# Attention context computed token by token, normalised once a layer, then transposed

## The reference, cut to what matters

```python
scores = jnp.einsum('bqhd,bkhd->bhqk', q, k) / scale     # layer 0: causal mask
attn = jax.nn.softmax(scores, axis=-1)
out = jnp.einsum('bhqk,bkhd->bqhd', attn, v).reshape(b, s, H * HS)
return out @ W_proj + b_proj
```

## Time and profile before

| what | us |
|---|---|
| median of 3 runs | 873.56 (868.95 to 879.3) |
| the profiled execution, its own time | 875.49 |
| its span, first to last instruction | 873.8 |
| mean granted TensorE clock in it | 0.846 of full |
| OPENING / FIRST / STEADY / STEADY / LAST / CLOSING, by barriers | 113.5 / 179.5 / 189.5 / 191.5 / 129.5 / 70.3 |

### The profile page before, as it was taken

One profiled execution on the slowest core, in us unless ns is written; L12 is line 12 of the kernel. 1 busy time (PEld: TensorE's weight loads), 2 busy tenths in 40 slices (PEclk: granted clock), 3 DMA queues, 4 the chain that ended last, 5 costly groups with the idle time before them and its releaser, 6 DMA issues. The chain is left out here.

```text
span 873.8 us, 8707 instructions
## 1 busy us (share of the span) xinstructions
PE 640.4 (73%) x3156; PEld 429.7 (49%) x3156; DVE 547.7 (63%) x936; ACT 307.6 (35%) x576; POOL 215.3 (25%) x184
## 2 busy tenths in 40 slices
PE   2479556835677787858778778857787888896697
PEld 2233234423223574646346565645345657765596
DVE  4749656576998547765997556757995355442211
ACT  2324031234331132653543223563442424442131
POOL 4429511212343101031543101132452011001000
PEclk9989965757888678888899788878998899998789
DMA  6985000354670000373660003273630000000000
GB/s 143 299 170 151 0 9 1 47 145 113 161 172 25 9 1 10 48 201 93 161 152 10 9 0 38 71 191 93 175 92 9 1 1 1 1 1 10 0 1 10
DMA packets 26641, 61.69 MB, mean 71 GB/s; under 512 B 4928, under 2 KB 12752, under 8 KB 26608
## 3 DMA queue, kind: packets, MB, share of 16 engines
q1 hardware_dynamic: 26608, 61.26, 30.2%
HBM read 53.52 MB, written 3.54 MB: 65 GB/s over the span
## 5 line engine op out<-in xcount | busy, mean ns | idle before, releaser
L1895 POOL TENSOR_TENSOR state<-state,C_rows 128x1024 f32<-128x1024 f32 x42 | 113.1, 2692 | 178.4 <-DVE state L1445 156.8
L1445 DVE TENSOR_TENSOR_SCAN state<-decay,dx_rows 128x512 f32<-128x512 f32 x72 | 105.8, 1510 | 9.9 <-PE py L980 6.9
L980 PE MATMUL py<-state,sel 128*96 128x512 f32 x168 | 91.9, 681 | 14.8 <-POOL state L1895 14.6
L1765 ACT ACTIVATE decay<-d_rows,a_neg 128x255 f32<-128x255 f32 x144 | 61.1, 496 | 94.5 <-DMA d_rows<-delta_dram 58.8
L1052 PE MATMUL pd<-w_dn,act 128*128 128x192 f32 x480 | 90.5, 343 | 3.7 <-ACT act L1778 3.7
L1052 PEld LDWEIGHTS pd<-w_dn,act 128*128 128x128 f32 x480 | 82.7, 200 | 7.1 <-ACT act L1778 4.6
L1036 PE MATMUL pu<-fT,w_up 128*128 128x256 f32 x180 | 65.9, 452 | 12.4 <-ACT act L1778 11.9
L1438 DVE TENSOR_TENSOR dx_rows<-dx_rows,B_rows 128x1024 f32<-128x1024 f32 x36 | 58.4, 1621 | 12.5 <-DMA dx_rows<-delta_x_dram 12.5
L792 PE MATMUL ps<-hT,w_qkv 96*96 96x256 f32 x128 | 41.5, 495 | 33.4 <-DVE hT L1583 32.7
L1936 POOL TENSOR_TENSOR cT<-cT,inv_den 128x256 f32<-128x256 f32 x24 | 19.9, 831 | 174.3 <-DVE inv_den L1642 174.3
L1778 ACT ACTIVATE act<-pu,b_up 128x256 f32<-128x256 f32 x90 | 37.7, 470 | 71.3 <-PE pu L1040 71.1
(11 more groups left out here) (285 smaller groups left out, 1220.0 us busy)
## 6 DMA issues: line engine op xcount, KB each, us to landing
dx_rows<-delta_x_dram SPq DMA_DIRECT2D x41, 512.0 KB, 5.1
d_rows<-delta_dram SPq DMA_DIRECT2D x36, 512.0 KB, 6.6
d_rows<-delta_x_dram SPq DMA_DIRECT2D x6, 512.0 KB, 5.1
w_dn<-exp_w_dram SPq DMA_DIRECT2D x1, 2304.0 KB
B_rows<-xdbl SPq DMA_DIRECT2D x4, 512.0 KB, 7.0
C_rows<-xdbl SPq DMA_DIRECT2D x4, 512.0 KB, 10.7
w_up<-exp_w_dram SPq DMA_DIRECT2D x1, 1536.0 KB
delta_x_dram<-delta_x SPq DMA_DIRECT2D x4, 384.0 KB, 3.4
```

The costliest lines, as they stand in the source:

```text
L980: mm = nc.tensor.matmul(py[0:INNER, :], sel[:, first:first + INNER], flat(states[g % held])[:, paths], start=False, stop=(g == GROUPS - 1) ...
L1445: ins = nc.vector.tensor_tensor_scan(flat(states[g % held])[:, both], flat(decay[g % 2])[:, both], dx_rows[g % 2][:, both], 0.0, ALU.mult, ...
L1765: ins = nc.scalar.activation(decay[g % 2][:, k, rest], d_rows[g % 2][:, k, rest], ACT.Exp, scale=a_neg[:, at:at + 1])
L1895: nc.gpsimd.tensor_tensor(now, now, C_rows[:, :], ALU.mult).then_inc(sc_done, 1)
```

## The change

The context is formed with tokens on the partitions. The stationary operand is a 128x128 tile of `probs` (keys x queries), the moving one 17 columns of `v_aug` (16 values and the ones). A head takes four products in layer 1 and three in the causal layer 0. All 24 x 17 columns of a layer stay in `pm` (408 of 512). After the last unit DVE takes one reciprocal of the 24 sums of each token and one product over 128x384; PE transposes the result with `turn`; DVE and ACT copy one half each to `cT`; the projection has two chunks of 96 rows. Gone are `den_sel`, `spread`, `context_copy`, `invert_sums`, `context_scale`, two memsets of `w_o`, and six of eight loads of `w_o`.

```diff
-            for j in range(QUAD):
-                b_loads.append((w_o[l][32 * j:32 * j + HEAD, :, :], w_heads[j]))
+            b_loads.append((w_o[l][:, :, :], t[f"w_o{l}"].rearrange("(c p) n -> p c n", p=CGROUP)))
...
                         def context(u):
                             pe.wait_ge(p_done[l], u + 1)
-                            if u in (2, 4):
-                                pe.wait_ge(den_inv[l], u // 2)
                             for j in range(2):
                                 head = 2 * u + j
-                                row = 32 * (head % QUAD)
-                                for kt in range(TILES):
-                                    q0 = 128 * kt if causal else 0
-                                    mm = nc.tensor.matmul(pm[row:row + 32, q0:TOKENS], v_aug[:, kt, head, :],
-                                                          probs[u % 2][:, j, kt, q0:TOKENS], ...
+                                for i in range(TILES):
+                                    out = pm[:, (HEAD + 1) * (HEADS * i + head):(HEAD + 1) * (HEADS * i + head + 1)]
+                                    tiles = range(i + 1 if causal else TILES)
+                                    for kt in tiles:
+                                        mm = nc.tensor.matmul(out, probs[u % 2][:, j, kt, 128 * i:128 * (i + 1)],
+                                                              v_aug[:, kt, head, 0:HEAD + 1],
+                                                              start=(kt == 0), stop=(kt == tiles[-1]))
...
-                            if u in (2, 4):
-                                spread(u // 2 - 1)
                             others((l, 2 * u + 1))
                         context(UNITS - 1)
                         others((l, "context"))
-                        spread(HTILES - 1)
+                        pe.wait_ge(ctx_done[l], 1)
+                        turn(pm, ps[:, 3, :], ctx_tok, CHALF).then_inc(ctx_turned[l], 1)
                         others((l, "spread"))
-                        pe.wait_ge(ctx_done[l], HTILES)
+                        pe.wait_ge(ctx_copied[l], 2)
                         for tl in range(TILES):
-                            for ht in range(HTILES):
-                                mm = nc.tensor.matmul(ps[:, 2, WIDTH * tl:WIDTH * (tl + 1)], ...
+                            mm = chunks(ps[:, 2, WIDTH * tl:WIDTH * (tl + 1)],
+                                        lambda c: cT[0:CGROUP, c, 128 * tl:128 * (tl + 1)],
+                                        lambda c: w_o[l][:, c, :])
...
+                        def normalise():
+                            dve.wait_ge(av_done[l], UNITS)
+                            context = pm[:, 0:TILES * HEADS * (HEAD + 1)].rearrange("p (t d) -> p t d", d=HEAD + 1)
+                            link(nc.vector.reciprocal(inv_den[:, :], context[:, :, HEAD]))
+                            nc.vector.tensor_tensor(
+                                ctx_tok[:, :, :].rearrange("p t (h d) -> p (t h) d", d=HEAD), context[:, :, 0:HEAD],
+                                inv_den[:, :].unsqueeze(2).to_broadcast([128, TILES * HEADS, HEAD]),
+                                ALU.mult).then_inc(ctx_done[l], 1)
...
-                            if u in (2, 4):
-                                context_copy(u // 2 - 1)
...
-                            if u in (2, 4):
-                                invert_sums(u // 2 - 1)
...
-                        context_copy(HTILES - 1)
+                        normalise()
                         others((l, "context"))
-                        invert_sums(HTILES - 1)
+                        dve.wait_ge(ctx_turned[l], 1)
+                        nc.vector.tensor_copy(cT[0:CGROUP, 0, :], pm[0:CGROUP, 0:TOKENS]).then_inc(ctx_copied[l], 1)
                         others((l, "spread"))
... (ACT)
                         others((l, "context"))
+                        sc.wait_ge(ctx_turned[l], 1)
+                        nc.scalar.activation(cT[0:CGROUP, 1, :], ps[0:CGROUP, 3, 0:TOKENS], ACT.Copy
+                                             ).then_inc(ctx_copied[l], 1)
                         others((l, "spread"))
... (POOL)
-                        if run_a and at in (5, 9, "spread"):
-                            context_scale(l, {5: 0, 9: 1, "spread": 2}[at])
```

More of the change, by code:

```diff
@@ L29 @@
 HEADS, HEAD = 12, 16
-QUAD = 4
-HTILES = HEADS // QUAD
 UNITS = HEADS // 2
@@ L400, in build @@
         sel = sb("sel", [128, INNER + GROUPS - 1])
-        den_sel = sb("den_sel", [128, QUAD, 32])
         dsum = sb("dsum", [INNER, 1])
@@ L421, in build @@
         top_one = sb("top_one", [128, 1])
-        w_o = [sb(f"w_o{l}", [128, HTILES, WIDTH]) for l in range(2)]
+        w_o = [sb(f"w_o{l}", [CGROUP, 2, WIDTH]) for l in range(2)]
         b_qk = [sb(f"b_qk{l}", [CGROUP, 2, 2]) for l in range(2)]
@@ L488, in build @@
         probs = [sb(f"probs{i}", [128, 2, 2, TOKENS]) for i in range(2)]
-        inv_den = sb("inv_den", [128, TOKENS])
-        cT = sb("cT", [128, HTILES, TOKENS])
+        inv_den = sb("inv_den", [128, TILES * HEADS])
+        ctx_tok = sb("ctx_tok", [128, TILES, WIDTH])
+        cT = sb("cT", [128, 2, TOKENS])
         x2 = sb("x2", [128, TILES, WIDTH])
@@ L605, in build @@
         ctx_done = [isem(f"context_ready{i}") for i in range(2)]
-        ctx_copied = [isem(f"context_copied{i}") for i in range(2)]
-        den_inv = [isem(f"sums_inverted{i}") for i in range(2)]
-        den_done = [isem(f"sums_spread{i}") for i in range(2)]
+        ctx_turned = [isem(f"context_turned{i}") for i in range(2)]
+        ctx_copied = [isem(f"context_T_copied{i}") for i in range(2)]
         proj_done = [isem(f"attention_projected{i}") for i in range(2)]
@@ L667, in build @@
             b_loads.append((w_qkv[l][:, :, :], w.rearrange("(c p) n -> p c n", p=CGROUP)))
-            w_heads = t[f"w_o{l}"].rearrange("(t j i) n -> j i t n", j=QUAD, i=HEAD)
-            for j in range(QUAD):
-                b_loads.append((w_o[l][32 * j:32 * j + HEAD, :, :], w_heads[j]))
+            b_loads.append((w_o[l][:, :, :], t[f"w_o{l}"].rearrange("(c p) n -> p c n", p=CGROUP)))
             b_loads.append((b_qk[l][:, :, :], b[0:2 * WIDTH].rearrange("(p c r) -> r p c", p=2, r=CGROUP)))
@@ L711, in _ @@
             def _(dve):
-                for buf in (w_o[0], w_o[1], w_gate, pad, gn_raw, gn_mv, gn_m):
+                for buf in (w_gate, pad, gn_raw, gn_mv, gn_m):
                     nc.vector.memset(buf[:], 0.0)
@@ L745, in attention_constants @@
         def attention_constants(link):
-            for tile, value in ((maskq, 0.0), (maskk, 0.0), (den_sel, 0.0), (lower, 1.0), (top_one, 0.0),
+            for tile, value in ((maskq, 0.0), (maskk, 0.0), (lower, 1.0), (top_one, 0.0),
                                 (cT, 0.0), (v_aug, 0.0)):
@@ L1192, in context @@
                             pe.wait_ge(p_done[l], u + 1)
-                            if u in (2, 4):
-                                pe.wait_ge(den_inv[l], u // 2)
                             for j in range(2):
                                 head = 2 * u + j
-                                row = 32 * (head % QUAD)
-                                for kt in range(TILES):
-                                    q0 = 128 * kt if causal else 0
-                                    mm = nc.tensor.matmul(pm[row:row + 32, q0:TOKENS], v_aug[:, kt, head, :],
-                                                          probs[u % 2][:, j, kt, q0:TOKENS],
-                                                          start=(kt == 0), stop=(kt == TILES - 1),
-                                                          tile_position=(0, row), skip_group_check=True)
-                            mm.then_inc(av_done[l], 1)
[L1206 to L1211, removed]
+                                for i in range(TILES):
[5 more added lines that the diff above has]
+                                                              start=(kt == 0), stop=(kt == tiles[-1]))
+                            mm.then_inc(av_done[l], 1)
                         scores(0)
```

6 lines of the change are left out of this document (removed).

## The result

The changed kernel takes **909.9 us** (906.45 to 914.13, four runs) beside 876.4 us for the kernel before in the same comparison: ratio 1.042, 95% interval [1.037, 1.047]. It is 4% slower; the forecast was 864.6 us, the range ended at 880. The profiled execution has a span of 906.6 us against 873.8. In what follows a time is the median of all runs of a kernel, while a ratio compares its fast runs alone (those within 1.5% of its fastest) with fast runs of the kernel before, so that the two can differ by a few tenths of a per cent.

The account below looks back on a forecast made before the run. Layer 1 with scans was taken as bound by DVE, layer 1 of LAST and layer 0 of STEADY by PE, layer 0 of FIRST by a chain through both. Terms -2.5 - 7.3 + 0.2 - 1.4 + 2 = -9.0 gave 864.6 us, range 850 to 880.

Parts of the forecast that it names:

- Price of a narrow product: PE's context products: a 17-column record steps at 0.113 us, as the 4-column gating product does; upper end 0.17.
- Rival B: Context products: 17-column records step like wide ones, at 0.17 us; +19 on the path, 884 us; chance 0.12.
- DVE: DVE per layer: reciprocals and copies off, 6.5 us; one reciprocal, product and half copy on, 1.3; net -5.2, -42 over eight.
- OPENING: Start of the kernel: fewer `w_o` issues on SP let the loads of rows B and C move up, -2.5 us.
- End of LAST: Layer 1 of LAST: the 2.87 us wait for POOL goes and the projection shortens (-2.5); layer sum -1.4 us.
- Layer 1 with scans: Three stretches: first copy and reciprocal and the tail saved, PE's contexts added; STEADY -2.0 twice, FIRST -3.3, sum -7.3 us.
- The added wait before the turn: Layer 0: PE's turn waits for last context, reciprocal and product; +1.3 us in FIRST, +0.3 in STEADY and LAST.
- together +0.2: Layer 0, four times: added contexts and wait against saved spreads and waits; +0.8 us for FIRST, -0.2 x 3.
- contexts that fall in low-clock parts: Contexts at the low clock cost 0.215 us a record, +0.8 each beyond the rest; about three on the path, +2 us.
- Rival D: Layer 1 of STEADY: with 17 columns the granted clock falls from 0.90 towards 0.75, gain gone, 873 us; chance 0.10.

Follow-up runs that it names:

- 104 columns: The changed kernel with each context product streaming 104 moving columns instead of 17, same records, token tiles of a head side by side in `pm`: 866.2 us, ratio 0.987.

## Why the prediction was wrong

- *Price of a narrow product, 0.113 us*: right, 0.112 (0.213 at the low clock). Rival B, which made the products dearer, is refuted; its time, 884, was the nearest, by luck: the cause is another.
- *DVE*: right in the added parts. Reciprocal, product and copy were forecast at 0.31, 0.56 and 0.42 us, and DVE's timeline in layer 0 of FIRST has

```profile
180.98 0.31 DVE L1619 RECIPROCAL inv_den<-pm 128x24 f32<-128x24 f32 x1 [6.66 <-PE pm L1191]
181.32 0.56 DVE L1620 TENSOR_TENSOR ctx_tok<-pm,inv_den 128x384 f32<-128x384 f32 x1
183.06 0.42 DVE L1637 COPY cT<-pm 96x256 f32<-96x256 f32 x1 [1.18 <-PE ps L777]
```

  The relief is 38.4 us, some 3.5 short of the forecast 42, because the scan's product took 63.6 us in 36 instructions, 58.4 before, and the scans 1.8 less; why was not followed up. Note the 6.66 us: DVE now waits for PE.
- *OPENING*: right, -2.4 for -2.5. The first scan group is 2.3 us sooner and its wait 2.3 shorter than in the earlier trace rows:

```profile
49.89 0.69 DVE L1401 TENSOR_TENSOR dx_rows<-ps,B_rows 128x512 f32<-128x512 f32 x1 [7.08 <-DMA C_rows<-xdbl]
```

- *End of LAST*: the wait of 2.87 us went, and the projection takes 1.57 us, 3.86 in the earlier trace rows. PE's timeline:

```profile
833.07 0.27 PE L777 MATMUL ps<-ident,ctx_tok 128*96 128x128 f32 x1
834.07 1.57 PE L784 MATMUL ps<-w_o,cT 96*128 96x192 f32 x8 [0.73 <-DVE cT L1637]
```

  The layer is still 1.5 us longer, for a forecast of -1.4: 16 of its 96 context records fell at the low clock, none before.
- *Layer 1 with scans*: STEADY -1.7 and -0.6 for -2.0 twice, FIRST +3.1 for -3.3. At 104 columns the layers give -1.5, -1.9, FIRST -3.9 and LAST -1.3 (forecast -1.4). So at 104 columns, with higher clocks in FIRST and LAST (0.79 for 0.66, 0.97 for 0.92), these terms come out near the forecast, which speaks for the path as it was read.
- *The added wait before the turn*: small, as forecast; 1.5 us of idle in all eight layers. It explains none of the 30 us.
- **The step that failed** is layer 0, "together +0.2", with the term beside it, "contexts that fall in low-clock parts ... about three on the path: +2". Both took the granted clock of layer 0 from the trace before and held it fixed. The measured term is +30 us: 184 of the 288 context records of layer 0, some 15 of 24 contexts, ran low, and with them the work between them. Rival D had the mechanism (17 columns instead of 256, the clock falls) and its sign came true (a granted clock below 0.82; it was 0.782), but it priced it for layer 1 of STEADY alone, at 873, and had 0.10. Its sum is also off: 15 us in each of two stretches, half on the path, are +15 on the -9.0, or 880. Layer 1 of STEADY was the one place that was safe; layer 0, bound by PE, with waits in it and clocks of 0.82 and 0.90 to lose, was where it had to be priced. At the 0.75 that the earlier trace rows show for another stretch, PE's 72 us there come to 72 x 0.82 / 0.75 = 79, in a layer that goes by PE; the clock came out at 0.72 and the busy time at 81.8. The kernel at 104 columns takes 866.2 us beside a forecast of 864.6, but that nearness is in part luck. Its layers 0 are 1.5 us longer in sum than before, about what was forecast, yet by +10.8, -0.3, -5.0 and -4.0: FIRST pays the low clock in full, and the others have clocks at or above those of the kernel before (0.82, 0.85, 0.95), which nothing in the forecast had.
- *All terms*: OPENING -2.4, layers 0 +30.3, layer 1 with scans +0.8, layer 1 of LAST +1.5, the late start of the second STEADY +3.1, CLOSING -0.5; together the 32.8 us between the two spans, where -9.0 was forecast.
- The Trainium skill, "TensorEngine Tiling (Array Packing)", Performance Considerations, advises against the new arrangement, and for the change as it was made the time agrees in direction (4% slower). What it says beside this, that a product of one column takes as long as one of sixty, agrees with the trace (a step of 0.112 us for 17 and for 60 columns), but that is a price the forecast had in it.

## What to carry to other kernels

Before a wide product is traded for narrow ones, take the stretches where PE sets the end and price PE's whole work in them at the clock that the thinner stream may get, not only the new products at their own step. See whether added moving columns lengthen the step at all: here 104 cost as much as 17, and bought 44 us. A short wait of PE ahead of such a stretch is a place for idle products, worth a try and no more than that: they gained 10 us here and nothing in the kernel before. With both, the form by tokens beats the kernel before by 1 to 3% (856.3 us, 0.981 [0.974, 0.988]).

## What the runs showed of the hardware

- PE can be busy without a gap for 16 us, by its records, and be granted 1.2 GHz throughout (160 to 176 in the changed kernel, and in the one with 104 columns). The Trainium skill, "TensorE: Matmul & The Clock Gate", Part 1, lets the clock follow how busy PE has been; the busy column of this trace, 8.00 of 8.00 us, did not bring the high clock.
- Kernels with the same records were granted different clocks in layer 0 of the first STEADY: 0.72 with 17 columns a product, 0.73 with 60, 0.82 with 104. With 17 columns it was 0.70 with two fillers of 168 columns ahead of each context and 0.86 with five. In layer 0 of FIRST 104 columns did not help in one execution (0.56) and did in another (0.63).
- The clock can differ by the execution: the same layer 0 of FIRST took 86.8 us in one kernel and 78.3 in another.
- With a 128x128 float32 stationary tile the step of a record was 0.112 us at the high clock for 17, 60 and 104 moving columns. With a tile of 128x32 eight records took 0.31 us together for 17 columns and 1.06 us for 256: there the columns set the step.
